# Cross-attention with layer norm on one core: a scale of v per group of batches, an earlier Wv, beta added in two parts, a residual ahead of a centring

## The chip, the cores and the metric

The kernel runs on one core of a Trainium2 chip. The metric is the time of one launch on the device in microseconds (us). Engines are named as in the profile: PE (TensorE; PEld its weight loads), ACT (ScalarE), DVE (VectorE), POOL (GpSimd), and SP, whose queue here issues every DMA. Each engine works through its own list of instructions in order; semaphores order the engines among each other.

## What is computed

x has 16 batches of 512 rows of 512 values, ctx 16 batches of 120 rows of 256. All in float32:

```python
q = einsum('bte,ef->btf', x, Wq) + bq
k = einsum('bml,le->bme', ctx, Wk) + bk
v = einsum('bml,le->bme', ctx, Wv) + bv
w = einsum('bte,bme->btm', q, k) / sqrt(512)
w = softmax(w, axis=1)              # over the 512 rows t
y = einsum('btm,bme->bte', w, v) + x
out = (y - mean(y)) * rsqrt(var(y) + 1e-6) * gamma + beta   # over e
```

## The kernel before

Wq and Wk are multiplied once (`multiply_qk`), so that of a batch's context only g, its product with them, is needed (`context_g`, for pairs of batches, on PE; `copy_g` on ACT brings it to SBUF as gT). The products with ctx, v and the probabilities run in float16 with a high and a low part each: ACT makes the high part (`..._to_high`), DVE the low part (`..._to_low`). Before the split a value is multiplied by a power of two, found from a bound of its size (`largest`, `bound_ctx`, a reduction over the partitions on POOL, then `exact_scales` on DVE). The context comes in four groups of four batches, with a scale for each; v has one scale for all batches, from the largest bound of the four groups, so that all of ctx must have been read before the first v is scaled.

The main loop runs over the 16 batches. In what follows step s is the pass of that loop (L444 on PE) in which x of batch s is transposed and scored, and T0(s) is the moment when PE begins it, which is the end of the scores of step s-1. PE's order in a step: two transposes of x (`turn_x`, L371), two row blocks of the product of probabilities and v of batch s-2 (`product`, L390), two transposes, two row blocks, `context_g` (L352), `context_v` of batch s-1 (L363), in odd steps the transposes of the next pair's context (`turn_ctx`, L336, four, before the scores), and `scores` (L400, eight matmuls).

ACT in a step: two copies of transposed x (L501), the exponential of batch s-1 (L506), `normalise` of row block 0 of batch s-3 (L534), the high part of the probabilities (L513), two copies of x, `normalise` of blocks 1 and 2, `copy_g` (L496), `square` of block 0 of batch s-2 (L528), in odd steps the context's high part (L488), the high part of v (L520), two more squares.

DVE in a step: softmax's largest value and bias (L680 to L689), the first residual, that is product times a scale plus x (L721), the reciprocal of softmax's sum (L694, L696), the centring of row block 3 of batch s-3 (L746), the second residual, the low part of the probabilities (L700), two residuals, `rescale` of block 3 (L754), v's scale and bias (`copy_v`, L706), statistics of block 3 (L727), low parts of ctx (L663, odd steps) and v (L711). PE's fourth row block of a product waits for the second residual, since both use bank b_ps, and `context_v` for the third, since both use a_ps.

POOL in a step: three multiplications with gamma (L925), each after ACT's `normalise` of its row block, one addition of beta over the three blocks (L931), then `finish_statistics` of batch s-2: a few small operations (L940 to L958) from the squares of ACT to 1/sqrt and shift, on which ACT's next `normalise` waits.

SP issues loads at the start in the order Wk, Wq, ctx 0, bk, bq, x 0, ctx 1, Wv, ctx 2, ctx 3, bv, x 1, x 2, gamma, beta, x 3. From then on (L288 to L296) it issues for each batch one load of x (1 MB, into a ring of four) and one store of a finished batch (1 MB), in this order:

```python
            for s in range(4, B + 2):
                if s < B:
                    sp.wait_ge(y_done, RJ * (s - 4) + RJ)
                    load_x(s)
                b = s - 4
                sp.wait_ge(pool_out, b + 1)
                sp.wait_ge(dve_out, dve_units_before(b + 1))
                sp.dma_start(out[b]...
```

So the load of x for step s+2 stands in the queue right behind the store of batch s-3.

Of the kernel before, what the change touches and what calls it, by code (L numbers as in the profile page):

```python
# [5 lines left out]
P = 128  # L6
# [8 lines left out]
XRING = 4  # L15
# [13 lines left out]
B_CTX0, B_WK, B_WQ0, B_WQ1, B_CTX1, B_WV = 0, 1, 2, 3, 4, 7  # L29

S_CTX0, S_QK, S_CTX1, S_WV, S_V = 0, 1, 2, 5, 6
# [7 lines left out]
def cross_attention(nc, x, ctx_in, Wq, bq, Wk, bk, Wv, bv, gamma, beta, out):  # L39
# [40 lines left out]
    with ExitStack() as stack:  # L80
# [36 lines left out]
        bound = sb("bound", [P, 7])  # L117
        field = sb("field", [P, 7])
        scale = sb("scale", [P, 7])
        back = sb("back", [P, 7])  # L120
# [3 lines left out]
        back_y = sb("back_y", [P, 1])  # L124
        bv_scaled = sb("bv_scaled", [P, E])
        ctx_nat = sb("ctx_nat", [M, B, L + 1])
        abs_ctx = sb("abs_ctx", [M, GROUPS - 1, IN_GROUP, L], F16)
# [46 lines left out]

        def v_bank(b):

            return cg_ps if b == B - 1 else a_ps
# [24 lines left out]
        own_late = sem("own_late")  # L202
# [4 lines left out]
        back_g_done = sem("back_g_done")  # L207
        wv_high = sem("wv_high")
# [51 lines left out]
        def _(sp):  # L260
# [15 lines left out]
            load_x(0)  # L276
            load_ctx(1)
            sp.dma_start(wv[:], Wv.rearrange("(c p) e -> p c e", p=P)).then_inc(wv_in, 16)
# [9 lines left out]
            for s in range(4, B + 2):  # L288
# [4 lines left out]
                sp.wait_ge(pool_out, b + 1)  # L293
# [14 lines left out]
        def _(pe):  # L308
# [20 lines left out]
            def turn_ctx(pair):  # L329

                if pair >= 2:
                    pe.wait_ge(g_copied, EC * pair)
# [41 lines left out]
            def product(b, j):  # L374
                if j == 0:
                    pe.wait_ge(prob_low, b + 1)
                    pe.wait_ge(v_low, b + 1)
# [16 lines left out]
            def scores(b):  # L394
# [49 lines left out]
            for s in range(1, B):  # L444
# [29 lines left out]
        def _(act):  # L474
# [16 lines left out]
            def copy_g(pair, half, ps):  # L491
                group = 2 * pair // IN_GROUP
                act.wait_ge(g_done, 2 * pair + half + 1)
# [22 lines left out]
            def v_to_high(b):  # L516
                act.wait_ge(v_copied, b + 1)
                if b >= 2:
                    act.wait_ge(pv_done, RJ * (b - 1))
                act.activation(v_part[:, b % 2, HIGH], v_bank(b)[0:M, :], ACT.Copy).then_inc(v_high, 1)  # L520
# [16 lines left out]
            def bound_ctx(g):  # L537
                act.wait_ge(ctx_in_sem[g], 16)
                act.activation(abs_ctx[:, g - 1], ctx_nat[:, g * IN_GROUP:(g + 1) * IN_GROUP, 0:L], ACT.Abs,
# [19 lines left out]
            bound_ctx(1)  # L559
# [3 lines left out]
            bound_ctx(2)  # L563
            copy_xT(0, 1)
            act.wait_ge(back_g_done, 1)
            act.wait_ge(dots_done, LC + 1 + EC)
            copy_g(0, 0, a_ps)
            copy_xT(0, 2)
            copy_xT(0, 3)
            copy_g(0, 1, b_ps)  # L570
            bound_ctx(3)

            for s in range(1, B):
# [6 lines left out]
                if s == 1:  # L580
                    act.wait_ge(scales_done, 2)
                    act.activation(wv_part[:, HIGH], wv[:], ACT.Copy, scale=scale[:, S_WV:S_WV + 1]).then_inc(wv_high, 1)
                probs_to_high(s - 1)
                copy_xT(s, 2)
                copy_xT(s, 3)
                if norm >= 0:
# [7 lines left out]
                if y >= 0:  # L594
                    square(y, 0)
                if s % 2 == 1 and (s + 3) // 2 < PAIRS:
                    ctx_to_high((s + 3) // 2)
                v_to_high(s - 1)
                if s == B - 1:
                    v_to_high(s)  # L600
# [27 lines left out]
        def _(dve):  # L628
# [74 lines left out]
            def copy_v(b):  # L703
                g = b // IN_GROUP
                dve.wait_ge(v_done, b + 1)
                dve.scalar_tensor_tensor(v_bank(b)[0:M, :], v_bank(b)[0:M, :], onto_v[0:M, g:g + 1], bv_scaled[0:M, :],  # L706
                                         ALU.mult, ALU.add).then_inc(v_copied, 1)

            def v_to_low(b):
                dve.wait_ge(v_high, b + 1)  # L710
# [3 lines left out]
            def residual(b, j):  # L714
                dve.wait_ge(pv_done, RJ * b + j + 1)
# [280 lines left out]
```

## Time and profile before

| | |
|---|---|
| time, median of 3 runs | 228.85 us (227.89 to 231.82) |
| time of the profiled execution | 228.07 us |
| its span | 226.2 us (1.87 us of the time lie around it) |
| busy share of the span | PE 84%, DVE 75%, ACT 72%, POOL 63% |
| TensorE's granted clock, mean | 0.957 of full speed |
| moved by DMA | 39.14 MB, 173 GB/s |

The profile is one execution. A busy share is an average over the start (to about 42 us), fifteen steps of 10.8 to 12.7 us, and the end from about 203 us. What sets the pace is read from the chain of waits, which follows the work that ended last back from the end, and from the timeline, which gives in brackets how long an engine sat idle before an instruction and what ended the idleness.

### The profile page before, as it was taken

The numbers are of one execution on the slowest core, as the hardware profiler recorded it, in microseconds if no ns is written. First come the engines' busy times: TensorE is split into PE (matmuls) and PEld (weight loads), VectorE is DVE, ScalarE is ACT, GpSimd is POOL, SyncE is SP. The second block draws the span as 40 slices with busy tenths as digits, with TensorE's granted clock in tenths as the row PEclk, the third lists the DMA queues.
The fourth block names the chain that finished last, engine by engine and source line by source line (L and its number), as shares of the span: only waits on it lengthen the run. The fifth ranks groups of instructions, "written<-read, shape, count | busy, mean of one in ns | idle before, by whom it ended". The sixth has DMA issues, their size and how long they took to land.

```text
span 226.2 us, 3278 instructions
## 1 busy us (share of the span) xinstructions
PE 190.5 (84%) x1003; PEld 117.6 (52%) x1003; DVE 169.3 (75%) x403; ACT 162.7 (72%) x336; POOL 142.0 (63%) x149
## 2 busy tenths in 40 slices
PE   6994998899996999999999999999999969696100
PEld 6993655465554565656565656555656535342000
DVE  0698138979899896959695969586958686879891
ACT  2745638378968797978797879787978876748730
POOL 1010005103994969696969696969696969698991
PEclk9999599999999999999999999999999999999855
DMA  5999940014018090909090909090909090404175
GB/s 220 315 313 250 398 198 1 3 14 172 0 81 293 0 346 28 352 22 351 23 355 17 352 19 351 23 336 36 348 26 352 19 351 25 185 0 187 67 294 197
DMA packets 9277, 39.14 MB, mean 173 GB/s; under 512 B 812, under 2 KB 2732, under 8 KB 5420
## 3 DMA queue, kind: packets, MB, share of 16 engines
q1 hardware_dynamic: 9260, 38.93, 49.0%
q8 instruction: 8, 0.13, 0.2%
q14 instruction: 9, 0.07, 0.1%
HBM read 22.15 MB, written 16.78 MB: 172 GB/s over the span
## 4 chain that ended last, share of the span: by engine, by line
PE 40%; POOL 16%; DVE 14%; ACT 9%; issue 8%; DMA 7%; SPq 2%; POOLq 1%; ACTq 0%; DVEq 0%
PE s_ps L400 16%; DMA ctx_nat<-in_ctx 7%; POOL obuf L925 7%; PE xT_ps L371 6%; POOL obuf L931 5%; PE a_ps L363 5%; PE a_ps L390 4%; PE b_ps L390 4%; DVE obuf L721 4%; PE cg_ps L352 4%; ACT xT L501 3%; ACT obuf L534 2%; POOL rstd L954 2%; ACT prob_part L513 2%; DVE obuf L746 2%
## 5 line engine op out<-in xcount | busy, mean ns | idle before, releaser
L925 POOL TENSOR_TENSOR obuf<-obuf,gamma_all 128x512 f32<-128x512 f32 x43 | 54.2, 1276 | 24.9 <-ACT obuf L534 24.9
L400 PE MATMUL s_ps<-xT,gT 128*120 128x512 f32 x128 | 58.9, 604 | 0.0
L931 POOL TENSOR_TENSOR obuf<-obuf,beta_all 128x1536 f32<-128x1536 f32 (+1 forms) x15 | 49.6, 3306 | 1.2
L501 ACT ACTIVATE xT<-xT_ps 128x512 f32<-128x512 f32 x64 | 34.6, 593 | 17.3 <-PE xT_ps L371 17.3
L534 ACT ACTIVATE obuf<-obuf,shift,rstd 128x512 f32<-128x512 f32 x43 | 33.4, 813 | 9.0 <-POOL shift L958 9.0
L371 PEld LDWEIGHTS xT_ps<-ident,xbuf 128*128 128x128 f32 x256 | 30.1, 142 | 15.1 <-issue 8.0
L371 PE MATMUL xT_ps<-ident,xbuf 128*128 128x128 f32 x256 | 34.0, 275 | 3.8 <-ACT xT L501 3.8
L400 PEld LDWEIGHTS s_ps<-xT,gT 128*120 128x120 f32 x128 | 23.5, 188 | 25.6 <-issue 23.7
L528 ACT ACTIVATE square_junk<-obuf,y_sum 128x512 f32<-128x512 f32 x46 | 32.8, 716 | 0.0
L390 PE MATMUL b_ps<-v_part,prob_part 120*128 120x512 f16 x90 | 24.5, 381 | 4.9 <-DVE obuf L721 4.9
L680 DVE TENSOR_REDUCE s_max<-s_ps 120x1 f32<-120x512 f32 x16 | 11.0, 689 | 20.3 <-PE s_ps L400 20.3
L390 PE MATMUL a_ps<-v_part,prob_part 120*128 120x512 f16 x90 | 24.4, 379 | 1.7 <-DVE v_part L711 0.9
L363 PE MATMUL a_ps<-wv_part,ctxT 128*120 128x512 f16 x90 | 22.0, 381 | 3.4 <-DVE obuf L721 3.1
L721 DVE SCALAR_TENSOR_TENSOR obuf<-a_ps,back_y,xbuf 128x512 f32<-128x512 f32 x30 | 22.4, 745 | 3.0 <-PE a_ps L390 3.0
L721 DVE SCALAR_TENSOR_TENSOR obuf<-b_ps,back_y,xbuf 128x512 f32<-128x512 f32 x30 | 22.3, 745 | 0.0
L352 PE MATMUL cg_ps<-ctxT,qk_part 128*128 128x240 f16 x156 | 18.1, 266 | 0.0
L390 PEld LDWEIGHTS b_ps<-v_part,prob_part 120*128 120x128 f16 x90 | 7.6, 97 | 19.1 <-DVE obuf L721 11.7
L706 DVE SCALAR_TENSOR_TENSOR a_ps<-a_ps,onto_v,bv_scaled 120x512 f32<-120x512 f32 x15 | 11.4, 758 | 8.2 <-PE a_ps L363 8.2
L954 POOL TENSOR_TENSOR rstd<-var_eps,minus_half 128x4 f32<-128x4 f32 x16 | 16.3, 1020 | 1.3 <-POOL var_eps L940 0.2
L352 PEld LDWEIGHTS cg_ps<-ctxT,qk_part 128*128 128x128 f16 x156 | 15.2, 98 | 3.5
L363 PEld LDWEIGHTS a_ps<-wv_part,ctxT 128*120 128x120 f16 x90 | 11.2, 133 | 10.1 <-issue 4.0
L700 DVE SCALAR_TENSOR_TENSOR prob_part<-s_ps,s_by,prob_part 120x512 f16<-120x512 f32 x16 | 12.0, 750 | 4.0 <-ACT prob_part L513 3.7
(142 smaller groups left out, 277.2 us busy)
## 6 DMA issues: line engine op xcount, KB each, us to landing
xbuf<-in_x SPq DMA_DIRECT2D x16, 1024.0 KB, 7.4
out<-obuf SPq DMA_DIRECT2D x14, 1024.0 KB, 4.8
out<-obuf SPq DMA_DIRECT2D x8, 256.0 KB, 2.8
ctx_nat<-in_ctx SPq DMA_DIRECT2D x4, 480.0 KB, 14.0
wq_nat<-in_L_xattn_Wq SPq DMA_DIRECT2D x2, 512.0 KB, 5.0
wk_nat<-in_L_xattn_Wk SPq DMA_DIRECT2D x1, 512.0 KB, 3.7
wv<-in_L_xattn_Wv SPq DMA_DIRECT2D x1, 512.0 KB, 14.3
bk_all<-in_L_xattn_bk SPq DMA_DIRECT2D x1, 256.0 KB, 7.6
```

Source lines behind the costliest of these rows:

```text
L352: mm = pe.matmul(ps[:, i * 2 * M:(i + 1) * 2 * M], qk_part[:, of_w, c, e * P:(e + 1) * P], ctxT[:, pair % 3, of_ctx, c, :], start=(n == 0) ...
L363: mm = pe.matmul(v_bank(b)[0:M, :], ctxT[:, b // 2 % 3, of_ctx, c, at:at + M], wv_part[:, of_w, c, :], start=(n == 0), stop=(n == len(step ...
L371: mm = pe.transpose(xT_ps[e % 2][:, j, :], xbuf[:, b % XRING, j, e * P:(e + 1) * P], ident[:])
L390: mm = pe.matmul(y_bank(b, j), prob_part[:, b % 2, of_p, j * P:(j + 1) * P], v_part[:, b % 2, of_v, :], start=(n == 0), stop=(n == len(PAS ...
L400: mm = pe.matmul(s_ps[0:M, :], gT[:, b // 2 % 2, e, b % 2 * M:(b % 2 + 1) * M], xT[:, e, :], start=(e == 0), stop=(e == EC - 1))
L501: act.activation(xT[:, e, :].rearrange("p (j q) -> p j q", q=P), xT_ps[e % 2][:], ACT.Copy)\
L528: act.activation(junk[:, j], obuf[:, b % ORING, j, :], ACT.Square, scale=-float(E), bias=y_sum[:, b % 2, j:j + 1], accum_out=square_sum[:, ...
L534: act.activation(obuf[:, b % ORING, j, :], obuf[:, b % ORING, j, :], ACT.Identity, bias=shift[:, b % 2, j:j + 1], scale=rstd[:, b % 2, j:j ...
L721: dve.scalar_tensor_tensor(obuf[:, b % ORING, j, :], y_bank(b, j), back_y[:], xbuf[:, b % XRING, j, :], ALU.mult, ALU.add, accum_out=y_sum ...
L925: pool.tensor_tensor(obuf[:, b % ORING, j, :], obuf[:, b % ORING, j, :], gamma_all[:], ALU.mult)\
L931: pool.tensor_tensor(obuf[:, b % ORING, 0:n, :], obuf[:, b % ORING, 0:n, :], beta_all[:].unsqueeze(1).broadcast_to([P, n, E]), ALU.add)\
L954: pool.tensor_tensor(rstd[:, k], var_eps[:], minus_half[:], ALU.pow).then_inc(rstd_done, 1)
```

## The change

- v gets a scale for each group of ctx. For group 0 it needs the bounds of ctx 0, Wv and bv only; the scales of groups 1 to 3 follow later, after the first v has been made. The bound of ctx 1 moves from ACT to DVE; those of ctx 2 and 3 stay on ACT, but move from the start into step 1. The scaled bias of v is then made once for each group.
- Wv and bv are loaded ahead of ctx 1, and x 1 ahead of ctx 2.
- beta is added in two parts: row blocks 0 and 1 before `finish_statistics`, block 2 after it. Each part counts `pool_out` up, and SP waits for both.
- DVE takes the second residual ahead of the centring.
- `turn_ctx` moves into the middle of the scores, and ACT and DVE take v's parts before ctx's.
- In step 15 v of the last batch is made before that of the batch ahead of it.
- POOL's multiplications for the keys wait until the scales are made (`back_v_done`).

```diff
             load_x(0)
+            sp.dma_start(wv[:], Wv...).then_inc(wv_in, 16)
+            sp.dma_start(bv_all[:], bv.partition_broadcast(P)).then_inc(bv_in, 16)
             load_ctx(1)
-            sp.dma_start(wv[:], Wv...).then_inc(wv_in, 16)
+            load_x(1)
             load_ctx(2)
             load_ctx(3)
-            sp.dma_start(bv_all[:], bv.partition_broadcast(P)).then_inc(bv_in, 16)
-            load_x(1)
...
-                sp.wait_ge(pool_out, b + 1)
+                sp.wait_ge(pool_out, 2 * (b + 1))
...  PE
+            def scores(b, next_pair=None):
                 for e in range(EC):
+                    if e == 2 and next_pair is not None:
+                        pe.wait_ge(ctx_in_sem[2 * next_pair // IN_GROUP], 16)
+                        turn_ctx(next_pair)
...
-                context_v(s - 1)
                 if s == B - 1:
                     context_v(s)
-                if s % 2 == 1 and (s + 3) // 2 < PAIRS:
-                    pe.wait_ge(ctx_in_sem[(s + 3) // IN_GROUP], 16)
-                    turn_ctx((s + 3) // 2)
-                scores(s)
+                context_v(s - 1)
+                scores(s, (s + 3) // 2 if s % 2 == 1 and (s + 3) // 2 < PAIRS else None)
...  ACT, start
-            bound_ctx(1)
             qk_to_high(3)
             ctx_to_high(1)
             copy_xT(0, 0)
-            bound_ctx(2)
             copy_xT(0, 1)
...
             copy_g(0, 1, b_ps)
-            bound_ctx(3)
+            act.wait_ge(wv_in, 16)
+            act.wait_ge(scales_done, 2)
+            act.activation(wv_part[:, HIGH], wv[:], ACT.Copy, scale=scale[:, S_WV:S_WV + 1])...
...  ACT, step 1: bound_ctx(2) ahead of probs_to_high(0), bound_ctx(3) behind copy_xT(1, 3)
...  ACT, every step
+                if s == B - 1:
+                    v_to_high(s)
+                v_to_high(s - 1)
                 if s % 2 == 1 and (s + 3) // 2 < PAIRS:
                     ctx_to_high((s + 3) // 2)
-                v_to_high(s - 1)
...  DVE, start: bounds of Wv, bv and ctx 1, scales of Wv and of v's group 0, then
+            softmax_bias(0)
             dve.wait_ge(wv_high, 1)
             dve.scalar_tensor_tensor(wv_part[:, LOW], ...
+            softmax_scale(0)
+            key_dot(1)
             probs_to_low(0)
+            copy_v(0)
+            v_to_low(0)
+            dve.wait_ge(max_bounds, 3)
+            ...                       # scales of groups 1 to 3, and ctx_to_low(2)
...  DVE, every step
                 softmax_scale(s - 1)
+                residual(y, 1)
                 if norm >= 0:
                     center(norm, RJ - 1, norm + 1)
-                residual(y, 1)
                 probs_to_low(s - 1)
...
+                v_to_low(s - 1)
                 if s % 2 == 1 and (s + 3) // 2 < PAIRS:
                     ctx_to_low((s + 3) // 2)
-                v_to_low(s - 1)
...
+                if s == 2:
+                    for g in range(1, GROUPS):
+                        dve.tensor_scalar(bv_scaled[:, g], bv_all[:], scale[...], None, ALU.mult)
...  POOL
+            pool.wait_ge(back_v_done, 5)
             key_multiply(1)
             key_multiply(2)
...
                     times_gamma(s - 3)
-                    plus_beta(s - 3)
+                    plus_beta(s - 3, 0, 2)
                 finish_statistics(s - 2)
+                if s >= 3:
+                    plus_beta(s - 3, 2, 3)
```

## Rows read from the trace of the kernel before

**Rows 1.** Timeline, POOL, one loop: start us, us, engine line op, tiles, [idle before].

```profile
135.08 0.20 POOL L940 TENSOR_SCALAR var_eps<-square_sum 128x3 f32<-128x3 f32 x1
...
138.00 1.27 POOL L925 TENSOR_TENSOR obuf<-obuf,gamma_all 128x512 f32<-128x512 f32 x1 [0.93 <-ACT obuf L534]
140.25 2.51 POOL L925 TENSOR_TENSOR obuf<-obuf,gamma_all 128x512 f32<-128x512 f32 x2 [0.98 <-ACT obuf L534]
142.83 3.46 POOL L931 TENSOR_TENSOR obuf<-obuf,beta_all 128x1536 f32<-128x1536 f32 x1
146.38 0.20 POOL L940 TENSOR_SCALAR var_eps<-square_sum 128x3 f32<-128x3 f32 x1
```

**Rows 2.** Stretches, steps 5 to 14: us, busy PE, PEld, DVE, ACT, POOL, clock, DMA.

```profile
78.00:190.00 112.00, 106.23 (x545) 62.60 (x543) 85.94 (x204) 92.28 (x192) 88.97 (x91) 1.00 0.53 188
```

**Rows 3.** Chain of waits, steps 7 and 8: start us, us, engine tile line.

```profile
108.00 0.60 PE cg_ps L336 x4
...
112.04 0.88 PE xT_ps L371 x8
...
119.41 3.43 PE s_ps L400 x8
```

**Rows 4.** Timeline, PE, its stalls in step 8 and in step 15.

```profile
116.06 0.82 PE L390 MATMUL b_ps<-v_part,prob_part 120*128 120x512 f16 x3 [0.32 <-DVE obuf L721]
...
196.59 1.48 PE L363 MATMUL a_ps<-wv_part,ctxT 128*120 128x512 f16 x6 [1.56 <-DVE obuf L721]
```

**Rows 5.** Timeline, the start to step 3: ACT, DVE and PE.

```profile
20.56 1.21 DVE L630 TENSOR_REDUCE own_bound<-wv 128x1 f32<-128x1024 f32 x1
21.35 1.06 ACT L539 ACTIVATE abs_ctx<-ctx_nat 120x1024 f16<-120x1024 f32 x1 [2.58 <-DMA ctx_nat<-in_ctx]
26.34 4.95 PE L400 MATMUL s_ps<-xT,gT 128*120 128x512 f32 x8
35.45 1.07 ACT L501 ACTIVATE xT<-xT_ps 128x512 f32<-128x512 f32 x2
36.40 1.00 ACT L496 ACTIVATE gT<-cg_ps,u_col,back_g 128x240 f32<-128x240 f32 x2
40.66 0.23 DVE L831 TENSOR_SCALAR onto_v<-back_v,scale 128x4 f32<-128x4 f32 x1
41.11 0.49 DVE L833 TENSOR_SCALAR bv_scaled<-bv_all,scale 128x512 f32<-128x512 f32 x1
41.64 0.43 DVE L675 SCALAR_TENSOR_TENSOR key_junk<-ctx_nat,w_row 120x257 f32<-120x257 f32 x1
44.01 0.68 DVE L680 TENSOR_REDUCE s_max<-s_ps 120x1 f32<-120x512 f32 x1
64.06 2.26 DVE L675 SCALAR_TENSOR_TENSOR key_junk<-ctx_nat,w_row 120x257 f32<-120x257 f32 x1
```

**Rows 6.** SP's issues in step 8, then loads by KB and us from issue to landing.

```profile
112.42 0.34 SPq L295 DMA_DIRECT2D out<-obuf  x1
112.81 0.50 SPq L262 DMA_DIRECT2D xbuf<-in_x  x1
...
xbuf<-in_x SPq DMA_DIRECT2D x16, 1024.0 KB, 7.4
...
xbuf<-in_x SPq DMA_DIRECT2D x1, 1024.0 KB, 4.8
...
xbuf<-in_x SPq DMA_DIRECT2D x1, 1024.0 KB, 8.6
```

**Rows 7.** Timeline, ACT in step 7, an odd step: context's high part, last square.

```profile
108.64 0.66 ACT L488 ACTIVATE ctxT<-cg_ps,scale 128x480 f16<-128x480 f32 x1
...
110.39 0.71 ACT L528 ACTIVATE square_junk<-obuf,y_sum 128x512 f32<-128x512 f32 x1
```

**Rows 8.** Timeline, the end: an addition on POOL and DVE's small operations beneath it.

```profile
209.84 3.44 POOL L931 TENSOR_TENSOR obuf<-obuf,beta_all 128x1536 f32<-128x1536 f32 x1
...
211.84 0.32 DVE L734 TENSOR_SCALAR mean<-y_sum 128x1 f32<-128x1 f32 x4
```

More of the change, by code:

```diff
@@ L116, in cross_attention @@
         bv_bound = sb("bv_bound", [P, 1])
[L117 to L120, printed above, removed]
+        bound = sb("bound", [P, 10])
+        field = sb("field", [P, 10])
+        scale = sb("scale", [P, 10])
+        back = sb("back", [P, 10])
         back_g = sb("back_g", [P, GROUPS])
@@ L207, in cross_attention @@
         back_g_done = sem("back_g_done")
+        back_v_done = sem("back_v_done")
         wv_high = sem("wv_high")
@@ L331, in turn_ctx @@
                 if pair >= 2:
-                    pe.wait_ge(g_copied, EC * pair)
+                    pe.wait_ge(g_copied, EC * pair if pair > 2 else EC + 2)
                 for c in range(LC):
@@ L492, in copy_g @@
                 group = 2 * pair // IN_GROUP
+                if pair == 2:
+                    act.wait_ge(back_g_done, 2)
                 act.wait_ge(g_done, 2 * pair + half + 1)
@@ L569, in _ @@
             copy_xT(0, 3)
+            act.wait_ge(dots_done, LC + EC)
             copy_g(0, 1, b_ps)
-            bound_ctx(3)
+            act.wait_ge(wv_in, 16)
+            act.wait_ge(scales_done, 2)
+            act.activation(wv_part[:, HIGH], wv[:], ACT.Copy, scale=scale[:, S_WV:S_WV + 1]).then_inc(wv_high, 1)
             for s in range(1, B):
@@ L580, in _ @@
                 if s == 1:
-                    act.wait_ge(scales_done, 2)
-                    act.activation(wv_part[:, HIGH], wv[:], ACT.Copy, scale=scale[:, S_WV:S_WV + 1]).then_inc(wv_high, 1)
+                    bound_ctx(2)
                 probs_to_high(s - 1)
@@ L585, in _ @@
                 copy_xT(s, 3)
+                if s == 1:
+                    bound_ctx(3)
                 if norm >= 0:
@@ L851, in _ @@
                     rescale(norm, RJ - 1)
+                if s == IN_GROUP + 1:
+                    dve.wait_ge(back_v_done, 2 + 3 + GROUPS - 1)
+                if s == B - 1:
+                    copy_v(s)
                 copy_v(s - 1)
                 statistics(y)
+                if s == B - 1:
+                    v_to_low(s)
+                v_to_low(s - 1)
                 if s % 2 == 1 and (s + 3) // 2 < PAIRS:
                     ctx_to_low((s + 3) // 2)
-                v_to_low(s - 1)
-                if s == B - 1:
-                    copy_v(s)
-                    v_to_low(s)
                 if s < IN_GROUP:
                     key_dot(s)
+                if s == 2:
+                    for g in range(1, GROUPS):
+                        dve.tensor_scalar(bv_scaled[:, g], bv_all[:], scale[:, S_V1 + g - 1:S_V1 + g], None, ALU.mult)\
+                            .then_inc(back_v_done, 1)
                 if s - 1 in (1, 2, 3):
@@ L926, in times_gamma, with plus_beta @@
                         .then_inc(pool_gamma, 1)
-            def plus_beta(b):
-                n = pool_units(b)
-                pool.wait_ge(pool_gamma, units_before(b + 1))
-                pool.tensor_tensor(obuf[:, b % ORING, 0:n, :], obuf[:, b % ORING, 0:n, :],
-                                   beta_all[:].unsqueeze(1).broadcast_to([P, n, E]), ALU.add)\
+            def plus_beta(b, first, end):
+                pool.wait_ge(pool_gamma, units_before(b) + end)
+                pool.tensor_tensor(obuf[:, b % ORING, first:end, :], obuf[:, b % ORING, first:end, :],
+                                   beta_all[:].unsqueeze(1).broadcast_to([P, end - first, E]), ALU.add)\
                     .then_inc(pool_out if b < B - 2 else last_out[b - B + 2][0], 1)
```

97 lines of the change are left out of this document (54 added, 43 removed).

## The prediction, made before the result was known

> **What bounds the kernel now.** I read the chain of waits first, then the timeline of each engine where the chain passes, then the stretches, then the DMA issues. At the start the chain hangs on the transfer of ctx 2: ACT stands 2.58 us before the bound of ctx 2, ahead of work that PE needs, so the scores of batch 0 begin only at 26.34, and the second softmax at 44.01 [rows 5]. In the loop the chain passes through POOL. One POOL loop takes 146.38 - 135.08 = 11.30, all of it work but two waits of 0.93 and 0.98 for ACT [rows 1]. PE is busy 106.23 of 112.0 us in steps 5 to 14, 10.6 a step [rows 2], so PE is the next limit and 0.6 away. The reader is to see that every later gain in the loop is capped at that.
>
> **The start.** In the new order nothing that waits for ctx stands ahead of ACT's copies of x 0: the wait of 2.58 and a bound of 1.06 go, so the scores of batch 0 begin at least 3.6 before 26.34, by 22.7 [rows 5]. They took 4.95 there, where PE had stood still before, and take 3.43 in the loop [rows 3, 5]: done by 26.1 at the latest. DVE then sets the pace: from 20.56 the bound of Wv (1.21), that of bv (half as many elements, about 0.7), one key product (0.43), the bound of ctx 1 (1.2, as Wv's), some nine dependent small operations at 0.2 each, and the scaled bias (0.49) [rows 5]: softmax of batch 0 begins near 26.4. From the scale of Wv (near 25.1) ACT has: Wv's high part 1.1, two copies of x 1.07, exponential and probabilities 1.4, two bounds at 1.2, two copies 1.07, four gT 2.0, v's high part 0.6 [rows 5], so it ends near 34.8. DVE's low part of v (0.7), eleven small operations for the other groups and ctx's low part (3.0 together) follow, and the second softmax starts at 38.5 instead of 44.01: **-5.5**. What is cheap here is so only while POOL is idle, which the new wait `back_v_done` sees to. Step 2 then carries three scaled biases on DVE, 3 x 0.49 = **+1.5**, ahead of softmax; they hide behind nothing. In step 3 a key product took 2.26 where it takes 0.43 elsewhere [rows 5], while POOL added beta; in the new order POOL is between its two parts then: **-1.8**. Bounds: 0 if POOL still adds, which is 1.8 later.
>
> **The loop, engine by engine.** beta's last part (one row block, 1.27 as one multiplication) lies in the 0.93 in which POOL waits for ACT anyway; the part ahead of the statistics is two thirds of 3.46, 2.3 [rows 1]. POOL's loop becomes 11.30 - 1.15 = 10.15 and is no longer the limit. The residual ahead of the centring takes away PE's stall of 0.32 before the fourth row block [rows 4]; the centring has slack, since the low probabilities wait for ACT. The four context transposes (0.60) [rows 3] now wait behind half the scores for gT, so ACT has that much longer; v's parts go ahead of ctx's at no cost, since ctx's are wanted only in the next step. Left to the engines, an even step takes 10.3 and an odd one 10.9, 21.3 a pair instead of 22.6, which over ten steps would be -6.
>
> **What is queued behind the new wait.** SP waits for both parts of beta before it stores batch s-3, and behind that store stands the load of x for step s+2. Before, that load was issued at 112.81, 0.8 into step 8 [rows 3, 6], and had until 122.8 for a median of 7.4. Now the last part comes after the statistics. In an odd step s, counted from T0(s): the scores begin at 119.41 - 112.04 = 7.4 less the stall and its restart [rows 3, 4], 6.9; half of them 1.7, the transposes 0.6: 9.2; ACT's context copy (0.6) and then two squares (0.71 and the read of the sum each) [rows 7]: 11.4. POOL's statistics take 138.00 - 0.93 - 135.08 = 2.0 [rows 1], beta's part 1.27, handovers 0.2: 14.9. The load follows 0.39 behind the store [rows 6] and takes 7.4: it lands at 22.7, and T0(s+2) is not before **22.8**. So one pair takes 22.8, where PE wants 21.3 and the old loop took 22.6. In even steps the squares are done at 9.8 and POOL itself sets the time: 10.3 + 2.0 + 1.4 = 13.7, landing at 21.5, hidden in a pair of 22.8. From T0(5) to T0(15) there are four such pairs and one without transposes (step 13), 21.5: 112.7 against 112.0 [rows 2]: **+0.7**. The gain of the engines is given back by the load. Bounds of the load: 4.8 with no store ahead of it, 8.6 the longest behind one [rows 6]; below 5.9 PE sets the pair, at 8.6 it is 24.0. I take the median, because the same store of 1 MB goes ahead of it as before.
>
> **The last step.** In step 15 PE stood 1.56 before `context_v` and 0.32 before the fourth block [rows 4]; v of batch 15 now fills the first, and with the restarts I take **-2.1**. The end behind the scores of batch 15 I cost at nothing: statistics of batch 14 come one part of beta sooner, but those of batch 15 wait for ACT's squares, and the last two row blocks for POOL as before. If that cover is gone, it is at most the 1.27 of one part.
>
> **Sum.** -5.5 + 1.5 - 1.8 + 0.7 - 2.1 = -7.2: span 226.2 - 7.2 = 219.0, with 1.87 around it 220.9, against 228.07 for the profiled execution. The median of the runs shown lies 0.3% above that execution, so I forecast **221.6** as a median.
>
> **A rule that speaks against it.** DVE's one-element operations of softmax now run while POOL adds or multiplies; before, POOL's small operations lay there. Four operations of that kind took 0.32 together in the middle of a POOL addition [rows 8], so I cost this at nothing. The Trainium skill (SBUF — State Buffer, "SBUF: two separate sides") says that a VectorE operation in a two-port mode and a GpSimd operation exclude one another for the whole instruction. If softmax's small operations took that mode, each could wait for the rest of an addition, and the sum would be that of the rival "port"; without it, it is the sum above. The rows bear out that the one-element form doesn't wait.
>
> **Rivals.**
> *Loads in time* (0.20). The load, or the squares, come 1.5 sooner in odd steps; PE then sets the pair. For it: 4.8 without a store. Against it: 7.4 and 8.6 behind one. Gain: 4 x (22.8 - 21.3) + (21.5 - 20.4) = 7.1 more, 213.8, as a median 214.5.
> *Long loads* (0.13). Each takes 8.6, 1.2 more in five pairs: +6.0, 226.9, median 227.6, no measurable change.
> *Still longer loads* (0.06), the other side. The mechanism is the queue: store and load are 2 MB, and each us that they take beyond 7.4 counts five times. At 7.4 + 7.2 / 5 = 8.8 nothing is left, and at 9.8 the kernel is 2% slower (233). Against it: none above 8.6 in the loop.
> *Port* (0.07). Softmax's one-element operations wait for POOL's part in either step; in odd steps up to 0.8, in even ones PE's slack hides it: 5 x 0.8 = 4.0, 224.9, median 225.7.
> *Start doesn't move* (0.10). DVE stands in order at the bound of ctx 1, whose transfer now follows Wv, bv and nothing that is shorter. Each us that it lands after 22.8 delays the first softmax by as much. With 5.5 lost: 226.4, median 227.2. Against it: Wv and bv are 0.75 MB, and before, the third group of ctx landed at 21.35 [rows 5] with 0.98 MB between x 0 and it.
> *The forecast* (0.44): 219 to 224.
>
> **Chances and range.** A difference of about 2%, 4.6 us, is what a measurement of this kernel can tell from no change. Faster than 224.3: the forecast and the loads in time, and little of the rest: 0.65. Within 2%: long loads, port, start: 0.29. Slower: 0.06. The range runs from 214 to 227, which leaves out the slowest case and the halves of the two that lie at its edges; the forecast's own is 219 to 224.
>
> **What would show it.** Right: the second softmax near 38.5; in POOL's timeline the last part of beta inside ACT's first `normalise`; PE idle 1 to 2 us before `turn_x` of odd steps only, waited for by the DMA of x; pairs of 22 to 24 us. If pairs take 21.3 with no wait for x, the load was hidden and the step "lands at 22.7" is wrong. If DVE's one-element operations show more than 0.5, it is the port. If DVE waits for the DMA of ctx before its bound, the start is wrong. My weakest number is 7.4: it is a median of transfers whose neighbours will have moved.

## The result and the profile after

| | before | after |
|---|---|---|
| time, median of 4 runs each | 228.84 us (227.89 to 231.82) | 215.26 us (214.94 to 218.25) |
| ratio of the times, 95% interval | | 0.9415 (0.9377 to 0.9454) |
| time and span of the profiled execution | 228.07 and 226.2 | 215.27 and 213.4 |
| granted clock of TensorE, mean | 0.957 | 0.969 |

The kernel became 13.6 us faster, where 7.2 were forecast; the time lies in the range of 214 to 227 and under the forecast's own 219 to 224. Cut at the starts of DVE's softmax (`s_max`), the two profiled executions compare so:

| stage | before | after | difference | forecast |
|---|---|---|---|---|
| to the second softmax | 44.01 | 36.86 | -7.15 | -5.5 |
| step 2 | 10.10 | 11.28 | +1.18 | +1.5 |
| step 3 | 13.27 | 11.70 | -1.57 | -1.8 |
| step 4 | 10.67 | 10.20 | -0.47 | 0 |
| steps 5 to 14 | 112.18 | 109.40 | -2.78 | +0.7 |
| step 15 | 12.60 | 10.74 | -1.86 | -2.1 |
| behind it | 23.37 | 23.22 | -0.15 | 0 |

The sum is -12.8, the difference of the spans. Two stages carry the miss: the start by 1.65 and the loop by 3.5. (Steps 2 to 4 of the kernel before took 10.10, 13.27 and 10.67; the 10.8 to 12.7 given for the steps above leaves these out.)

The start, from the timeline of DVE of the kernel after (start us, us, engine line op, tiles, idle before):

```profile
20.57 1.21 DVE L642 TENSOR_REDUCE own_bound<-wv 128x1 f32<-128x1024 f32 x1
21.70 0.68 DVE L642 TENSOR_REDUCE bv_bound<-bv_all 128x1 f32<-128x512 f32 x1
...
22.63 1.22 DVE L823 TENSOR_REDUCE own_bound<-ctx_nat 120x1 f32<-120x1024 f32 x1
...
25.52 0.68 DVE L692 TENSOR_REDUCE s_max<-s_ps 120x1 f32<-120x512 f32 x1
...
33.71 0.69 DVE L723 SCALAR_TENSOR_TENSOR v_part<-a_ps,v_part 120x512 f16<-120x512 f32 x1 [1.52 <-ACT v_part L528]
...
36.86 0.69 DVE L692 TENSOR_REDUCE s_max<-s_ps 120x1 f32<-120x512 f32 x1
```

The reader is to see that no bracket of the first four rows names a DMA: Wv, bv and ctx 1 are there when DVE comes to them. The wait of 2.58 in [rows 5] has no counterpart, and TensorE no longer stands still ahead of the first scores. Page rows of the granted clock, 40 slices, in tenths: first the kernel before,

```profile
PEclk9999599999999999999999999999999999999855
```

then the kernel after:

```profile
PEclk9999999999999999999999999999999999999755
```

Before, the fifth slice ran at half speed, the lower of TensorE's two levels, after a stand of 3.55 us (timeline of PE of the kernel before); the scores of batch 0 took 4.95 there [rows 5] and 3.60 after.

```profile
23.04 1.12 PE L371 MATMUL xT_ps<-ident,xbuf 128*128 128x128 f32 x4 [3.55 <-ACT xT L501]
```

A second loss of the old start stands neither in the rows above nor in the sum. Two operations of DVE on three elements a partition took 1.60 and 2.00; each ended 0.02 to 0.03 behind one of POOL's two multiplications for the keys, of 2.18 each (timeline of POOL and DVE of the kernel before):

```profile
36.27 4.32 POOL L911 TENSOR_TENSOR key_product<-ctx_nat,w_row 120x1028 f32<-120x1028 f32 x2 [7.11 <-issue]
36.87 1.60 DVE L825 TENSOR_SCALAR back_g<-back 128x3 f32<-128x3 f32 x1
38.62 2.00 DVE L829 TENSOR_SCALAR back_v<-back 128x3 f32<-128x3 f32 x1
```

In the kernel after, where `back_v_done` holds them, POOL's multiplications begin at 38.90, behind the second softmax. Neither loss is in every execution of the old start. The run with beta's split alone (below) has the start of the kernel before, and in its profile, where POOL's first maximum and the work behind it came 2.6 later, PE stood 2.27 instead of 3.55, the clock stayed at 1.00, the two operations of DVE took 0.22 and 0.23, and the second softmax came at 40.03 instead of 44.01. Of these 3.98, 2.5 lie ahead of the end of batch 0's scores and 1.5 where DVE was late. So the -7.15 hangs by some us on which execution of the kernel before was profiled; by medians, the start alone brought 6.7.

The loop, from the waits of PE after (us in total, times, longest) and its timeline:

```profile
PE xT_ps L376 <- DMA xbuf<-in_x: 3.2, 4, 0.9
```

```profile
92.21 1.09 PE L376 MATMUL xT_ps<-ident,xbuf 128*128 128x128 f32 x8 [0.88 <-DMA xbuf<-in_x]
...
114.32 1.09 PE L376 MATMUL xT_ps<-ident,xbuf 128*128 128x128 f32 x8 [0.76 <-DMA xbuf<-in_x]
...
136.37 1.09 PE L376 MATMUL xT_ps<-ident,xbuf 128*128 128x128 f32 x8 [0.70 <-DMA xbuf<-in_x]
...
158.54 1.09 PE L376 MATMUL xT_ps<-ident,xbuf 128*128 128x128 f32 x8 [0.83 <-DMA xbuf<-in_x]
```

PE waits for x ahead of `turn_x` of steps 7, 9, 11 and 13, odd ones only, as forecast, but 0.7 to 0.9 instead of 1 to 2. What it waits for ahead of step 11 began in step 9 (timeline of PE, ACT, POOL and SP after):

```profile
122.98 0.58 PE L341 MATMUL cg_ps<-ident,ctx_nat 120*128 120x120 f32 x4
123.59 0.66 ACT L494 ACTIVATE ctxT<-cg_ps,scale 128x480 f16<-128x480 f32 x1 [0.74 <-PE cg_ps L341]
...
124.86 0.71 ACT L536 ACTIVATE square_junk<-obuf,y_sum 128x512 f32<-128x512 f32 x1
...
125.75 0.20 POOL L975 TENSOR_SCALAR var_eps<-square_sum 128x3 f32<-128x3 f32 x1 [1.13 <-ACT square_junk L536]
...
127.70 1.27 POOL L966 TENSOR_TENSOR obuf<-obuf,beta_all 128x512 f32<-128x512 f32 x1
...
129.00 0.34 SPq L300 DMA_DIRECT2D out<-obuf  x1
129.38 0.43 SPq L267 DMA_DIRECT2D xbuf<-in_x  x1
```

Transposes, context copy, squares, statistics, beta's last part, store, load: the chain of the forecast. The load took 7.0 and set 136.37. POOL, whose loop of 11.30 had no other waits than two of 0.93 and 0.98 [rows 1], now stands 1.13 for ACT's squares: it is no longer the limit.

### The profile page after: what moved, and what is told of

It is laid out like the page before. It is cut to its first block and busy times, and to the rows that moved or that the text cites. A ratio compares the mean times of both kernels' runs of the same rounds, so it can differ in the third digit from the quotient of the medians.

```text
span 213.4 us, 3310 instructions
## 1 busy us (share of the span) xinstructions
PE 186.2 (87%) x1003; PEld 117.0 (55%) x1003; DVE 166.1 (78%) x413; ACT 161.5 (76%) x334; POOL 143.3 (67%) x164
## 5 line engine op out<-in xcount | busy, mean ns | idle before, releaser
L966 POOL TENSOR_TENSOR obuf<-obuf,beta_all 128x512 f32<-128x512 f32 (+1 forms) x29 | 52.1, 1796 | 0.1
L376 PEld LDWEIGHTS xT_ps<-ident,xbuf 128*128 128x128 f32 x256 | 29.3, 141 | 16.7 <-DMA xbuf<-in_x 8.9
L409 PEld LDWEIGHTS s_ps<-xT,gT 128*120 128x120 f32 x128 | 22.9, 183 | 22.4 <-issue 19.5
L542 ACT ACTIVATE obuf<-obuf,shift,rstd 128x512 f32<-128x512 f32 x43 | 33.7, 823 | 1.2 <-POOL shift L993 1.2
L368 PE MATMUL a_ps<-wv_part,ctxT 128*120 128x512 f16 x90 | 22.1, 381 | 1.1 <-DVE obuf L734 1.1
L395 PEld LDWEIGHTS b_ps<-v_part,prob_part 120*128 120x128 f16 x90 | 8.4, 97 | 12.7 <-DVE obuf L734 3.0
L514 ACT ACTIVATE s_ps<-s_ps,s_bias 120x512 f32<-120x512 f32 x16 | 10.7, 668 | 5.1 <-DVE s_bias L701 5.0
## 6 DMA issues: line engine op xcount, KB each, us to landing
wv<-in_L_xattn_Wv SPq DMA_DIRECT2D x1, 512.0 KB, 10.8
```

Of the source, the lines that this page charges most:

```text
L368: mm = pe.matmul(v_bank(b)[0:M, :], ctxT[:, b // 2 % 3, of_ctx, c, at:at + M], wv_part[:, of_w, c, :], start=(n == 0), stop=(n == len(step ...
L376: mm = pe.transpose(xT_ps[e % 2][:, j, :], xbuf[:, b % XRING, j, e * P:(e + 1) * P], ident[:])
L395: mm = pe.matmul(y_bank(b, j), prob_part[:, b % 2, of_p, j * P:(j + 1) * P], v_part[:, b % 2, of_v, :], start=(n == 0), stop=(n == len(PAS ...
L409: mm = pe.matmul(s_ps[0:M, :], gT[:, b // 2 % 2, e, b % 2 * M:(b % 2 + 1) * M], xT[:, e, :], start=(e == 0), stop=(e == EC - 1))
L542: act.activation(obuf[:, b % ORING, j, :], obuf[:, b % ORING, j, :], ACT.Identity, bias=shift[:, b % 2, j:j + 1], scale=rstd[:, b % 2, j:j ...
L966: pool.tensor_tensor(obuf[:, b % ORING, first:end, :], obuf[:, b % ORING, first:end, :], beta_all[:].unsqueeze(1).broadcast_to([P, end - f ...
```

## The experiments

Times are medians. The runs stand in three series, each with its own runs of the kernel before: 228.5, 227.5 and 229.52 us. Of the last series no ratio is given, since its runs of the kernel before scatter: one of 223.5 at a mean granted clock of 0.972, six of 227.6 to 230.3 at 0.940 to 0.957. Stages come from one profile of each kernel, with the load ahead of the store from its second taking. Four profiled executions lie over 1 us off the median beside them: split alone 220.76, beta not split 222.88, late Wv 219.95, centring first 218.35.

| kernel | time | ratio (interval) | second softmax | steps 5 to 14 | step 15 |
|---|---|---|---|---|---|
| after | 215.26 | 0.942 (0.938 to 0.945) | 36.86 | 109.40 | 10.74 |
| load ahead of store | 211.29, again 211.11 | 0.926 (0.922 to 0.929) | 36.92 | 105.33 | 10.37 |
| squares first | 213.83 | 0.938 (0.934 to 0.942) | 37.46 | 106.82 | 10.75 |
| load ahead, squares first | 212.07 | 0.931 (0.925 to 0.937) | 37.59 | 105.46 | 10.37 |
| beta not split | 221.20 | 0.971 (0.965 to 0.976) | 39.05 | 112.55 | 11.28 |
| the start alone | 221.82 | 0.971 (0.967 to 0.975) | 36.95 | 112.04 | 12.58 |
| late Wv, bv and x 1 | 218.84 | 0.960 (0.953 to 0.967) | 42.22 | 108.67 | 10.74 |
| beta's split alone | 223.41 | 0.979 (0.971 to 0.988) | 40.03 | 110.39 | 11.64 |
| v's order in step 15 undone | 217.46 | 0.956 (0.951 to 0.962) | 37.46 | 108.99 | 11.99 |
| load ahead, centring first | 216.26 | | 38.94 | 109.38 | 10.86 |
| transposes ahead of scores | 213.75 | | 37.38 | 107.29 | 10.75 |
| x 1 last | 216.50 | | 38.06 | 109.08 | 10.73 |

**Is the load of x, queued behind the store, the loop's limit?** The load is issued ahead of the store:

```diff
+            sp.wait_ge(y_done, RJ)
+            load_x(4)
             for s in range(4, B + 2):
-                if s < B:
-                    sp.wait_ge(y_done, RJ * (s - 4) + RJ)
-                    load_x(s)
+                if s + 1 < B:
+                    sp.wait_ge(y_done, RJ * (s - 3) + RJ)
+                    load_x(s + 1)
```

> The changed kernel, with the load of x for step s+2 one place ahead of the store in SP's queue; it then waits only for its own ring slot. Theory (the load behind the store sets a pair of steps at 22.1 us): PE's waits of 0.7 to 0.9 us for the DMA of x ahead of steps 7, 9, 11 and 13 vanish, pairs become about 21.3 (PE busy 106.2 over ten steps of the kernel before), so 3 to 3.5 us less: 211.5 to 212.5. Rival (engines: the wait for x only stands where another wait would, for example ACT's squares in odd steps or POOL's loop): pairs stay near 22, 214.5 to 215.5.

> The changed kernel with the load of x one place ahead of the store in SyncE's queue, taken a second time for its profile. Theory (TensorE waits for nothing in the loop any more and its own work sets the pair): 211.3 us, 210.8 to 211.8; steps 5 to 14 take 105.4 to 105.6, 21.1 a pair, and no row of TensorE there names the transfer of x. Rival (the loads now land in time in most steps only): 105.8 to 107, with a wait for x in one or two odd steps.

Measured: 211.29 and 211.11, about 4 us less than after and a little under the first theory's band. Stretches, steps 5 to 14 (us, busy PE, PEld, DVE, ACT, POOL, clock, DMA), first of the kernel after, then of this one:

```profile
80.81:190.18 109.37, 104.96 (x535) 62.30 (x534) 85.79 (x206) 91.50 (x192) 90.79 (x101) 1.00 0.52 183
```

```profile
80.84:185.80 104.96, 103.87 (x535) 62.72 (x534) 85.77 (x206) 91.59 (x192) 90.59 (x101) 1.00 0.48 181
```

The transfers (KB, median us from issue to landing) in the same order:

```profile
xbuf<-in_x SPq DMA_DIRECT2D x16, 1024.0 KB, 6.9
...
out<-obuf SPq DMA_DIRECT2D x14, 1024.0 KB, 4.8
```

```profile
xbuf<-in_x SPq DMA_DIRECT2D x16, 1024.0 KB, 5.0
...
out<-obuf SPq DMA_DIRECT2D x14, 1024.0 KB, 3.9
```

The work is the same, and PE is now busy in 103.87 of 104.96 us; its waits name the transfer of x nowhere, and pairs take 21.1. The theory holds: the place in the queue cost the kernel after about 4 us.

**Can the chain ahead of the store be shortened instead?** ACT's last two squares go ahead of the context's high part in odd steps from 3:

```diff
-                if s % 2 == 1 and (s + 3) // 2 < PAIRS:
-                    ctx_to_high((s + 3) // 2)
+                if s == 1:
+                    ctx_to_high(2)
...
                     square(y, 1)
                     square(y, 2)
+                if s >= 3 and s % 2 == 1 and (s + 3) // 2 < PAIRS:
+                    ctx_to_high((s + 3) // 2)
```

> The changed kernel, with ACT's two last squares of an odd step ahead of the context's high part, SP's queue as it is. Theory (the pair is the chain transposes of ctx, ACT's context copy, squares, statistics, second part of beta, store, load): the chain of an odd step gets about 1 us shorter, so PE's waits for x nearly vanish and pairs fall to 21.3 to 21.5: 212 to 213. Rival (the load is late because of the transfer itself, not of when it is issued): 215. Rival (context's parts become late instead, DVE waits for them ahead of softmax): 215 to 217.

Measured: 213.83, above the theory's band. Steps 7 to 12 came down to 21.1 a pair, as expected; two things ate part of it. In step 3 DVE stood 1.23 instead of 0.68 for the context's high part, and softmax came 0.57 later. And one load of x took 8.4 instead of about 6.9: step 13 took 11.63 with a wait of 1.1.

> The changed kernel with two edits that were each run alone (211.29 and 213.83 us): the load of x stands one place ahead of the store in SyncE's queue, and ScalarE squares its last two row blocks ahead of ctx's high part in odd steps. Theory (with the load ahead of the store nothing in the loop waits for x any more, and TensorE's own work of about 21.1 us a pair of steps is the limit): the sooner squares have nothing left to bring, 211.3 us, 210.8 to 211.8. Rival 1 (part of what the load of x cost is still there with the load ahead, so the two gains add in part): 209.0 to 210.5. Rival 2 (ctx's high part behind the squares makes ctx and gT late; the run with the squares alone had a step 13 of 11.6 and a step 3 of 12.3): 212.0 to 213.0, and TensorE waits for ctxT or gT in odd steps. In its profile, by the theory, TensorE waits for the transfer of x in no step from 5 to 14.

Both edits together: 212.07, by the medians no better than the load alone. That lies 0.3 over the theory's band, at the lower edge of rival 2's. The loop takes 105.46, where it took 105.33 with the load alone, and PE waits for x in no step of it: of the loop the theory holds, since once PE sets the pair, sooner squares have nothing to bring. Step 3 takes 12.25 (11.70 with the load alone); that cost is the one rival 2 named.

**Which move made the squares late?** Transposes ahead of the scores and context parts ahead of v's, as before the change:

```diff
-                scores(s, (s + 3) // 2 if s % 2 == 1 and (s + 3) // 2 < PAIRS else None)
+                if s % 2 == 1 and (s + 3) // 2 < PAIRS:
+                    pe.wait_ge(ctx_in_sem[(s + 3) // IN_GROUP], 16)
+                    turn_ctx((s + 3) // 2)
+                scores(s)
...  ACT and DVE: ctx's parts ahead of v's
```

> The changed kernel with one move undone: the transposes of ctx stand ahead of the scores again, and ScalarE and VectorE take ctx's parts ahead of v's, as before. The queue of SyncE is that of the changed kernel (load behind the store). Theory (it is the move of the transposes behind half of the scores that makes ScalarE's last squares late in odd steps, and with them statistics, beta's last part, store and load): the squares end about 1.2 sooner in odd steps, the pair falls from 22.1 to 21.1 plus what TensorE stands for gT ahead of the transposes (0.33 and its restart), 21.4; 212.3 to 213.0 us, and the wait for the transfer of x is gone or below 0.3. Rival (the squares are late for another reason, the chain behind the split): 215.0 to 215.6 us with the same wait for x. Second rival (the stall for gT costs as much as the load did): 215 with no wait for x.

Measured: 213.75, a little above the band. Pairs take 21.27, with no wait for x in steps 7, 9 and 11. One of 1.12 is left, in step 13, and in this kernel too one long load was the cause (timeline of PE; then the loads of x issued at 137.59, 147.95 and 158.87):

```profile
156.51 1.09 PE L376 MATMUL xT_ps<-ident,xbuf 128*128 128x128 f32 x8 [1.12 <-DMA xbuf<-in_x]
```

```profile
xbuf<-in_x SPq DMA_DIRECT2D x1, 1024.0 KB, 6.9
...
xbuf<-in_x SPq DMA_DIRECT2D x1, 1024.0 KB, 8.5
...
xbuf<-in_x SPq DMA_DIRECT2D x1, 1024.0 KB, 6.9
```

ACT's squares end 10.3 behind T0 in odd steps here, 11.3 in the kernel after. So the moves of the transposes and of v's parts, themselves part of the change, put the load of x on the path: with this queue they cost 0.8 a pair. Which of the two did it was not tried apart.

**What does the split of beta carry?** Undone in the kernel after, and alone in the kernel before:

```diff
-                sp.wait_ge(pool_out, 2 * (b + 1))
+                sp.wait_ge(pool_out, b + 1)
...
-                    plus_beta(s - 3, 0, 2)
+                    plus_beta(s - 3, 0, 3)
                 finish_statistics(s - 2)
-                if s >= 3:
-                    plus_beta(s - 3, 2, 3)
```

> The changed kernel, with beta added in one piece ahead of the statistics as before. Theory (POOL's loop was the limit and the split is what lifted it): POOL's loop of about 11.3 us returns, steps 5 to 14 take 112 to 113 instead of 109.4: 218 to 219. Rival (the residual ahead of the centring and the later context transposes shortened the loop, the split only moved the store back): pairs of 21.3 to 22, 213 to 215.

Measured: 221.20, 2 us above what was expected. POOL's loop is back in full (timeline of POOL, this kernel):

```profile
107.87 0.20 POOL L975 TENSOR_SCALAR var_eps<-square_sum 128x3 f32<-128x3 f32 x1
...
110.79 1.27 POOL L961 TENSOR_TENSOR obuf<-obuf,gamma_all 128x512 f32<-128x512 f32 x1 [0.93 <-ACT obuf L542]
...
115.63 3.44 POOL L966 TENSOR_TENSOR obuf<-obuf,beta_all 128x1536 f32<-128x1536 f32 x1
119.16 0.20 POOL L975 TENSOR_SCALAR var_eps<-square_sum 128x3 f32<-128x3 f32 x1
```

119.16 - 107.87 = 11.29, as before [rows 1], with the same 0.93 for ACT. Steps 5 to 14 take 112.55, step 3 0.8, step 15 0.5 and the end 0.9 more than after. (In this profile POOL's first maximum came 2.3 us late; that shifts the start and none of these. The same shift of about 2 us stands in the second softmax of "centring first".)

> The kernel before with one part of the change alone: beta's addition in two parts around the statistics, the store waiting for both; start, order of residual and centring and step 15 as before. Theory (POOL's loop of 11.3 was the limit of the loop and the split takes it away; then the load of x behind the store sets pairs of about 22.1 us instead of 22.6): steps 5 to 14 take 109.4 to 110.2 instead of 112.0, the key product of step 3 falls from 2.26 to 0.42, step 15 stays at 12.6; together -3.5 to -4.5: 224.4 to 225.4 us, ratio 0.983. Rival 1 (the stall of 0.32 before the fourth row block, which the order of residual and centring takes away, holds the loop as well): steps 5 to 14 at 111.5 to 112.0, 226.5 to 227.2 us. Rival 2 (all of the loop's gain came from the sooner start of the x loads, and the split only moves beta): 228.5 us, ratio 1.00.

Measured: 223.41, a ratio as expected, with an interval that reaches to 0.988. But the reason was not the expected one: PE waits for x once only, 0.73 ahead of step 13, behind a load of 8.6. Each step holds the stall before the fourth row block (timeline of PE), and each pair up to there takes 22.08:

```profile
109.36 0.81 PE L390 MATMUL a_ps<-v_part,prob_part 120*128 120x512 f16 x3
110.49 0.82 PE L390 MATMUL b_ps<-v_part,prob_part 120*128 120x512 f16 x3 [0.32 <-DVE obuf L721]
```

From block to block it is 1.13, where it is 0.65 without the stall: 0.48 a step, and 21.1 + 2 x 0.48 = 22.06. And step 3's key product took 1.04, not 0.42, because POOL's first part of beta still ran (timeline of POOL and DVE):

```profile
58.78 2.36 POOL L930 TENSOR_TENSOR obuf<-obuf,beta_all 128x1024 f32<-128x1024 f32 x1
...
60.39 1.04 DVE L675 SCALAR_TENSOR_TENSOR key_junk<-ctx_nat,w_row 120x257 f32<-120x257 f32 x1
```

It ends 0.3 behind POOL's addition. The Trainium skill (SBUF — State Buffer, "SBUF: two separate sides") names this case: a VectorE operation with two inputs in SBUF excludes a GpSimd operation that reads SBUF, and the later one waits. The trace agrees, here and in the 2.26 of before [rows 5]. The second softmax at 40.03 is no work of the split: its start is the old one, which came out quicker in this execution, as said above.

**What is the second residual ahead of the centring worth?** Undone, with the load ahead of the store:

```diff
...  SP as in the run with the load ahead of the store; DVE:
-                residual(y, 1)
                 if norm >= 0:
                     center(norm, RJ - 1, norm + 1)
+                residual(y, 1)
```

> The load of x ahead of the store, as in the run of that name, and the order of residual and centring put back (centring ahead of the second residual). In the run with the split of beta alone TensorE stood 0.32 before the fourth row block in every step, and from the start of the third block to that of the fourth went 1.13 instead of 0.65. Theory (the stall is on the path as soon as TensorE is the limit): 0.48 a step, 4.8 over steps 5 to 14, and up to 1.5 in steps 3, 4 and 15: 216.1 to 217.6 us against 211.3. Rival (the second residual is wanted late enough, VectorE's order only moves a wait): 211.3 to 211.8. A value between would say that part of the stall is given back in even steps.

Measured: 216.26, 5 us more than with the load alone. The stall is back:

```profile
110.50 0.82 PE L397 MATMUL b_ps<-v_part,prob_part 120*128 120x512 f16 x3 [0.32 <-DVE obuf L736]
```

Steps 5 to 14 take 109.38 instead of 105.33, 0.4 a step. The theory holds. It is also the same 109.4 as after, from another wait.

**Step 15.** v of batch 15 behind v of batch 14 again, on PE, ACT and DVE:

```diff
+                context_v(s - 1)
                 if s == B - 1:
                     context_v(s)
-                context_v(s - 1)
...  ACT and DVE likewise
```

> The changed kernel with the order of v in step 15 put back on TensorE, ScalarE and VectorE (v of batch 14 before v of batch 15). Theory (v of batch 15 fills a stall before context_v, as in the kernel before, where TensorE stood 1.56 there): step 15 takes 12.0 to 12.6 instead of 10.74, everything else stays, 216.6 to 217.2 us, ratio 0.948. Rival (step 15 became shorter because POOL's loop is no longer late when it begins, and the stall before context_v is gone with that or hidden): step 15 stays at 10.7 to 11.0, 215.3 to 215.6 us, ratio 0.942.

Measured: 217.46, a little above the band; step 15 takes 11.99, at its lower edge, and the end 0.46 more than after. PE stands again, now 1.07, ahead of `context_v`:

```profile
185.38 1.48 PE L368 MATMUL a_ps<-wv_part,ctxT 128*120 128x512 f16 x6 [1.07 <-DVE obuf L734]
```

**The start.** After's start with the loop, the order of DVE and step 15 of before:

> The changed kernel's start (a scale for each group, Wv and bv sooner, bounds of ctx 2 and 3 in step 1) with the loop of the kernel before: beta in one part, residual behind the centring, context transposes ahead of the scores, context's parts ahead of v's, v of batch 14 ahead of batch 15. Theory (start worth 7 to 8 us up to the scores of step 4, loop and end worth the rest, 4.8): 220 to 221. Rival (part of the 8 us is earned by the loop's edits in steps 2 to 4): 222 to 223.

Measured: 221.82, between the two bands. The second softmax comes at 36.95, the loop takes 112.04. So the start carries about half of the 13.6 us, the other edits the rest. Next, Wv behind ctx 1, and bv and x 1 behind ctx 3, as before:

```diff
-            sp.dma_start(wv[:], Wv...).then_inc(wv_in, 16)
-            sp.dma_start(bv_all[:], bv.partition_broadcast(P)).then_inc(bv_in, 16)
             load_ctx(1)
-            load_x(1)
+            sp.dma_start(wv[:], Wv...).then_inc(wv_in, 16)
             load_ctx(2)
             load_ctx(3)
+            sp.dma_start(bv_all[:], bv.partition_broadcast(P)).then_inc(bv_in, 16)
+            load_x(1)
```

> The changed kernel with one thing put back: Wv is loaded behind the second group of ctx and bv behind the fourth, as before; everything else of the change stays. In the kernel before, with that order, VectorE stood 2.33 us for bv and bounded it at 24.09; in the changed kernel it bounds it at 21.70 without a wait. Theory (the sooner loads carry part of the start's gain, because the scale of v of group 0 needs the bound of bv and VectorE stands in order): the wait is back, the first softmax comes 2.4 later (27.9 instead of 25.5), the second one at 39.2 instead of 36.9, and nothing behind it gives that back: 217.6 us, ratio to the kernel before 0.951. Rival (the start's gain comes from ScalarE's order and the smaller scale alone; the later bv is covered by the wait for POOL's maximum or by ScalarE): the second softmax stays at 36.9 to 37.4, 215.3 to 215.8 us, ratio 0.942. A value over 218.5 would say that later loads of x 1 cost besides.

Measured: 218.84, beyond the theory. The wait for bv is back, but the second softmax moved by 5.4, 0.9 of it from work ahead of Wv's bound. Timeline of DVE and PE, then stretches (us, busy PE, PEld, DVE, ACT, POOL, clock, DMA):

```profile
25.05 0.69 DVE L642 TENSOR_REDUCE bv_bound<-bv_all 128x1 f32<-128x512 f32 x1 [2.39 <-DMA bv_all<-in_L_xattn_bv]
...
27.56 1.09 PE L376 MATMUL xT_ps<-ident,xbuf 128*128 128x128 f32 x8 [2.27 <-DMA xbuf<-in_x]
29.79 1.97 PE L376 MATMUL xT_ps<-ident,xbuf 128*128 128x128 f32 x8 [1.14 <-ACT xT L509]
31.55 2.61 PE L357 MATMUL cg_ps<-ctxT,qk_part 128*128 128x240 f16 x12
```

```profile
28.00:32.00 4.00, 2.86 (x17) 2.47 (x16) 3.55 (x13) 3.74 (x6) 0.00 (x0) 0.62 0.88 356
32.00:36.00 4.00, 4.00 (x23) 3.08 (x22) 0.90 (x3) 3.67 (x9) 0.38 (x1) 0.53 0.02 10
```

The first softmax came 3.4 later: 2.4 of it is the wait for bv, 0.9 the work ahead. The other 2.0 fell between the two softmaxes: PE stood 2.27 and 1.14, came back at the lower level for most of 8 us (the product with the context took 2.61 instead of 1.39 at full clock), and v came late. Of the two late transfers, the next run moves x 1 alone:

```diff
             load_ctx(1)
-            load_x(1)
             load_ctx(2)
             load_ctx(3)
+            load_x(1)
```

> The changed kernel with one load moved: x 1 behind the third and fourth group of ctx instead of ahead of them; Wv and bv stay where the change put them. In the run with Wv and bv late, x 1 was the last one too, TensorE stood 2.27 for it, and the clock of the following 8 us was 0.62 and 0.53 instead of 1.00. Theory (the late x 1, not only the late bv, sets the second softmax, and TensorE comes back at the lower clock): VectorE bounds bv without a wait and the first softmax stays at 25.5 to 26.2; TensorE waits about 2 for x 1, the second softmax comes 2 to 4.5 later than 36.9, and 217.3 to 219.5 us. Rival (bv's wait alone moved the second softmax in that run; x 1 is covered by ScalarE's high part of Wv): 215.2 to 216.0 us.

Measured: 216.50, between theory and rival. PE waits 1.36 for x 1, the clock stays at 1.00, and the second softmax comes 1.20 later:

```profile
26.56 1.09 PE L376 MATMUL xT_ps<-ident,xbuf 128*128 128x128 f32 x8 [1.36 <-DMA xbuf<-in_x]
```

So x 1's place alone costs 1.2. What of the 2.0 in the run before is the wait for x 1, what the lower clock and what ACT's later Wv was not taken apart.

## Why the prediction was right and wrong

- **"The start: -5.5"**: right that ACT's wait goes and that DVE and ACT then set the pace, short by 1.65. Two terms were too dear. ACT's list from Wv's high part to v's, which I let run from 25.1 to 34.8, ran from 24.74 to 33.7, 1.1 sooner; behind it I charged 3.7 for DVE, and 33.71 to 36.86 is 3.15. The scores of batch 0 began at 21.24, not by 22.7, at full clock, and the first softmax at 25.52, not 26.4, without a wait for them. What the sum did not have: the 44.01 from which it starts held the lower clock and the hold by POOL, 4 us that another execution of the same start did without. The wait `back_v_done`, which I named as what keeps DVE's operations cheap, is borne out by the 1.60 and 2.00 of before. "Start doesn't move" fell: no wait for ctx 1.
- **"3 x 0.49 = +1.5"**: the three biases took 1.27 together, the step 1.18 more. **"Step 3: -1.8"**: the key product took 0.42, the step 1.57 less.
- **"POOL's loop is no longer the limit"**: right; the runs without the split and with it alone show both sides.
- **"The residual takes away PE's stall of 0.32"**: right, but under-sized. It is 0.48 from start to start, 4 us over the loop where PE is the limit, and the 0.47 of step 4, for which the sum had nothing.
- **"v's parts go ahead of ctx's at no cost"**, and the transposes behind half the scores as a gain for ACT: this step failed. My own chain behind SP's wait ran through those transposes, and I didn't ask what it would be without the move. The run with both undone shows it 1.1 shorter and pairs of 21.27.
- **"The load lands at 22.7, T0(s+2) is not before 22.8"**: mechanism, place and steps right, and the size of a term wrong. Step 9 gives the store at T0 + 14.7 (forecast 14.9), the load 0.38 behind it, 7.0 for the load (forecast 7.4) and T0(11) at + 22.05, 0.75 less than forecast. More than half of that is the load: its 7.4 was a median over 16 transfers, those of the start among them. The loads of the loop behind a store took 6.9 to 7.3; those of the kernel before, taken alone, have a median of 7.1. The rest are handovers and the allowance behind the landing. There are four such pairs, as forecast (T0 of steps 7, 9, 11 and 13 at 92.21, 114.32, 136.37 and 158.54), and the pair without transposes took 21.0 instead of 21.5: 4 x 0.7 + 0.5 = 3.3 of the 3.5 us.
- **Rivals**: "Loads in time" came near in time (214.5 for 215.26), but its mechanism isn't what happened: the loads were late in four steps. That the time lies in the range is partly luck: it lies there because the range takes in part of this rival. "Long loads" did not occur in the kernel after. "Port" fell: in the kernel after, softmax's one-element operations take 0.16, just ahead of POOL's addition of beta (`s_rec`) and 0.03 into it (`s_by`) alike (timeline of DVE and POOL):

```profile
105.43 0.16 DVE L706 RECIPROCAL s_rec<-s_sum 120x1 f32<-120x1 f32 x1
...
105.59 1.28 POOL L966 TENSOR_TENSOR obuf<-obuf,beta_all 128x512 f32<-128x512 f32 x1
...
105.62 0.16 DVE L708 TENSOR_SCALAR s_by<-s_rec 120x1 f32<-120x1 f32 x1
```

  That holds for one element: the two operations on three elements in the start of the kernel before did end with POOL's.
- **"Step 15: -2.1"**: -1.86; undoing v's order gave 1.25 back in that step. The remainder, 0.6, is near the 0.49 by which centring first lengthened step 15 (10.86 against 10.37), that is the stall before the fourth block. **The end, 0**: -0.15.

## What to carry to other kernels

Limits lie close above one another in a tuned loop: here POOL's loop (22.6 a pair), DVE's order (22.1) and a load behind a store (22.1) stood over PE's own 21.1, and each fix paid only down to the next. A load that is needed soon does not belong behind a store that waits for late work: exchanging two lines in the queue gave the 4 us that the change had left, and the fastest of all kernels here, 211.1 to 211.3 us. Price a transfer by those of its own stretch, not by a median over the kernel.

## What was not expected of the hardware

- Store and load of 1 MB each, the load 0.38 behind the store: 4.8 and 6.9 from issue to landing. With the load ahead, which then follows the last store by 2.3 and more: 3.9 and 5.0. Both had moved out of each other's way.
- Single loads of x of 8.1 to 8.6 stand among neighbours of 6.8 to 7.8 in six profiles: at 135.4 and 158.0 us in the kernel before, at 130.8 and 153.4 without the split, at 128.6 and 151.2 with the start alone, at 153.5 with the split alone, and at about 148 with the squares first (8.4) and with the transposes ahead (8.5). The kernel after has none. The cause stays open.
- The lower clock of PE followed a stand of 3.55 (before), and stands of 2.27 and 1.14 with 1.1 of work between (late Wv). Behind a stand of 2.27 (split alone), and behind stands of 1.36 and 0.25 (x 1 last), the granted clock stayed at 1.00.
- DVE's operations on three elements a partition ended with POOL's multiplication (1.60 and 2.00 us, where they took 0.22 and 0.23 with POOL idle); one-element operations beside POOL's additions kept their 0.16.
- In one execution, 1115.74 us long, each matmul of the scores took 3.08 with the load ahead of the store; in the second taking of the same kernel it was 0.59. DVE's largest value took 0.69 in both. The cause stays open.
